# Moving and spreading the placing of a score table, with two score buffers, in a one-core recommendation kernel

## The reference, cut to what matters

```python
ub = jnp.concatenate([table_i1[rec_his[:, :, 0]], table_i2[rec_his[:, :, 1]], table_i3[rec_his[:, :, 2]]], axis=2)
mask = rec_his[:, :, 0] == 0
q = jnp.broadcast_to(item_emb[:, None, :], ub.shape)
att_in = jnp.concatenate([q, ub, q - ub, q * ub], axis=-1)
score = ((att_in @ w_att1.T + b_att1) @ w_att2.T + b_att2)[..., 0]
score = jnp.where(mask, 0.0, score)
browse = jnp.einsum('bl,ble->be', score, ub)
feat = jnp.concatenate([item_emb, browse, user_emb], axis=-1)
x = _dice(feat @ w1.T + b1, a1, g1, be1)      # _dice: mean and variance over the batch
x = _dice(x @ w2.T + b2, a2, g2, be2)
return jax.nn.sigmoid(x @ w3.T + b3)[:, 0]
```

## Time and profile before

| | us |
|---|---|
| three runs | 1587.96, 1591.98, 1605.28 |
| median | 1591.98 |
| the profiled execution, own time | 1586.62 |
| its span | 1584.8 |
| mean granted TensorE clock | 0.921 |
| DVE busy | 1438.4 (91%) |
| PE busy | 1328.5 (84%) |
| POOL busy | 1131.4 (71%) |
| ACT busy | 717.1 (45%) |

### The profile page before, as it was taken

One profiled execution on the slowest core, in us unless ns is written; L12 is line 12 of the kernel. 1 busy time (PEld: TensorE's weight loads), 2 busy tenths in 40 slices (PEclk: granted clock), 3 DMA queues, 4 the chain that ended last, 5 costly groups with the idle time before them and its releaser, 6 DMA issues.

```text
span 1584.8 us, 67332 instructions
## 1 busy us (share of the span) xinstructions
PE 1328.5 (84%) x26911; PEld 1224.4 (77%) x26911; DVE 1438.4 (91%) x1453; ACT 717.1 (45%) x1633; POOL 1131.4 (71%) x1669
## 2 busy tenths in 40 slices
PE   5687989889797988979788797888989798887965
PEld 4576878778796887869788797888879797787861
DVE  7799999999999898999989899898999999899955
ACT  5353544536354453525435353453535355352217
POOL 3588788787878787776766768587787878677830
PEclk8799999999899998999999899999999899898966
DMA  2778676675857686584676758567686856668730
GB/s 30 146 109 159 104 146 124 130 149 111 168 100 151 108 137 134 111 167 95 138 111 128 147 111 154 92 141 131 111 167 112 151 107 144 118 115 157 117 70 0
DMA packets 510281, 194.21 MB, mean 123 GB/s; under 512 B 484005, under 2 KB 491797, under 8 KB 510045
## 3 DMA queue, kind: packets, MB, share of 16 engines
q1 hardware_dynamic: 492454, 162.61, 57.2%
q10 hardware_dynamic: 15448, 26.51, 6.5%
q0 software_dynamic: 2144, 1.36, 0.8%
HBM read 8.45 MB, written 1.44 MB: 6 GB/s over the span
## 4 chain that ended last, share of the span: by engine, by line
POOL 58%; issue 24%; DVE 6%; PE 5%; DMA 2%; POOLq 2%; SPq 2%; ACT 1%; DVEq 0%; ACTq 0%
POOL score L431 16%; POOL score L436 13%; POOL score_r L440 10%; POOL parts L441 6%; POOL parts L444 6%; POOL parts L437 3%; POOL item_rows L409 2%; DMA hiT<-onehot_hi 2%; POOL user_rows L417 2%; PE sel L532 1%; DVE score_j L999 1%; DVE onehot_hi L967 1%; DVE scaled_lo L1011 1%; PE wsum_ps L549 1%; PE misc L637 1%
## 5 line engine op out<-in xcount | busy, mean ns | idle before, releaser
L532 PE MATMUL sel<-scoretab,hiT 128*128 128x75 bf16 x12288 | 560.3, 206 | 142.8 <-DMA hiT<-onehot_hi 116.8
L532 PEld LDWEIGHTS sel<-scoretab,hiT 128*128 128x128 bf16 x12288 | 521.3, 103 | 204.1 <-issue 147.2
L549 PE MATMUL wsum_ps<-scaled_lo,onehot_hi 100*128 100x75 bf16 x12288 | 554.3, 204 | 73.8 <-DVE scaled_lo L1011 73.7
L549 PEld LDWEIGHTS wsum_ps<-scaled_lo,onehot_hi 100*128 100x128 bf16 x12288 | 509.4, 102 | 89.9 <-DVE scaled_lo L1011 83.8
L1011 DVE TENSOR_TENSOR scaled_lo<-onehot_lo,parts 100x3744 bf16<-100x3744 bf16 x256 | 539.4, 2107 | 24.0 <-POOL parts L444 20.0
L754 ACT ACTIVATE wsum_ring<-wsum_ps 128x300 f32<-128x300 f32 x512 | 215.5, 421 | 674.7 <-PE wsum_ps L549 668.1
L431 POOL TENSOR_TENSOR score<-score_j 100x16 f32<-100x16 f32 x256 | 310.4, 1213 | 293.4 <-DVE score_j L999 292.6
L999 DVE TENSOR_REDUCE score_j<-sel 100x24 f32<-100x600 f32 x512 | 395.8, 773 | 34.7 <-PE sel L532 34.0
L967 DVE TENSOR_TENSOR onehot_hi<-digits,iota_hi 100x1920 bf16<-100x1920 bf16 x256 | 297.5, 1162 | 45.9 <-PE wsum_ps L549 45.4
L761 ACT ACTIVATE scores_b<-acc 128x512 bf16<-128x512 f32 (+1 forms) x318 | 256.1, 805 | 44.9 <-PE acc L568 23.7
L436 POOL TENSOR_TENSOR score<-score,score_j 100x16 f32<-100x16 f32 x256 | 229.7, 897 | 22.0
(11 more groups left out here) (155 smaller groups left out, 663.5 us busy)
## 6 DMA issues: line engine op xcount, KB each, us to landing
scoretab<-scores_b SPq DMA_DIRECT2D x144, 187.5 KB
weightsum<-wsum_ring ACTq DMA_DIRECT2D x128, 125.0 KB
weightsum<-wsum_ring ACTq DMA_DIRECT2D x64, 150.0 KB
scoretab<-scores_b SPq DMA_DIRECT2D x96, 93.8 KB
raw<-in_r_rec_his_dram SPq DMA_DIRECT2D x32, 150.0 KB
hiT<-onehot_hi SPq DMA_TRANSPOSE x256, 4.5
x_rows<-x_tile SPq DMA_DIRECT2D x14, 100.0 KB
scores_b<-x_rows SPq DMA_DIRECT2D x1, 1400.0 KB
```

The costliest lines, as they stand in the source:

```text
L532: mm = pe.matmul(sel[:, 2 * (s % 2) + q, (c % 4) * W:(c % 4 + 1) * W] .rearrange("p (j v) -> p j v", j=NF), hiT[0:HJ, s // 2 % 4, g * POSP ...
L549: mm = pe.matmul(wsum_ps[:, s % 2, b * W:(b + 1) * W].rearrange("p (j v) -> p j v", j=NF), hi_columns(ring_slot(n), g), scaled_lo[:, n % 2 ...
```

## The change

- The chunks are all 16 users (`CHUNK = 16`, eight a tile), and `scoretab` holds four of them in turn (`HELD = 4`, 64 users in all, half of what it held). Chunks 0 and 1 of tile t+1 are placed in steps 14 and 15 of tile t, and chunks 2 to 7 in steps 0, 2, 4, 6, 8 and 10 of tile t+1, each behind that step's transpose. This is 24 DMAs a tile in place of 15, with the same bytes.
- `scores_b` has two buffers, for even and odd tiles. ACT's first copy waits only for the chunks of the tile before.
- Splitting stands in slots 2 to 10 (rounds 0 to 2) and 16 to 27 (rounds 3 to 6), and not in slots 11 to 15. The last piece is in slot 27, as it was.
- PE's program is written out for all 16 tiles; SP and ACT loop over pairs of tiles, since the buffer alternates. DVE and POOL keep their loops.
- DVE clears half as many bytes ahead of tile 0 and fills the constant rows by 12 copies of 16 users in place of 6 of 64. In the tail two scratch tiles lie elsewhere.

```diff
-        scoretab_flat = sb("scoretab", [128, 2 * NF * HALF * 3 * LO], BF16)
+        scoretab_flat = sb("scoretab", [128, HELD * NF * CHUNK * 3 * LO], BF16)
-        scores_flat = sb("scores_b", [HJ, TILE * 3 * LO], BF16)
+        scores_flat = sb("scores_b", [HJ, 2 * TILE * 3 * LO], BF16)
...
-        ROWS = (0, 16, 32, 64, 96, 128)
-        CHUNKS = len(ROWS) - 1
         for r, (l0, l1) in enumerate(ROUNDS):
             for piece in ("all", 1, 2):
-                split_at[7 + len(split_at)] = (r, piece)
+                split_at[len(split_at) + (2 if r < 3 else 7)] = (r, piece)
...
-            def place_scores(t, c):
-                await_ge(split_copied, SPLIT_DONE * (t + 1))
-                b0, b1 = ROWS[c], ROWS[c + 1]
-                if isinstance(t, int) and t == 0:
-                    sp.wait_ge(scoretab_zero, b0 // HALF + 1)
+            def place_scores(t, c, odd):
+                g = CHUNKS * t + c
+                if c == 0:
+                    await_ge(split_copied, SPLIT_DONE * (t + 1))
+                if isinstance(g, int) and g < HELD:
+                    sp.wait_ge(scoretab_zero, c // 2 + 1)
                 else:
-                    await_ge(sel_full, SLOTS * t - (SLOTS - b1 // 4))
+                    await_ge(sel_full, (CHUNK // 4) * (g - HELD + 1))
...
-                    if n == 14 and not last:
-                        place_scores(t + 1, 0)
+                    if n >= 14 and not last:
+                        place_scores(t + 1, n - 14, 1 - odd)
                     if n + AHEAD < STEPS:
                         turn_hi(t, n + AHEAD)
                     elif not last:
                         turn_hi(t + 1, n + AHEAD - STEPS)
-                    if n < 2:
-                        place_scores(t, 3 + n)
+                    if n % 2 == 0 and n // 2 + 2 < CHUNKS:
+                        place_scores(t, n // 2 + 2, odd)
...
-            for c in range(3):
-                place_scores(0, c)
+            for c in range(2):
+                place_scores(0, c, 0)
...
-                if 4 * s in ROWS:
-                    pe.wait_ge(scoretab_in[ROWS.index(4 * s)], (t + 1) * (NF * 16))
+                chunk = 4 * s // CHUNK
+                if 4 * s % CHUNK == 0:
+                    pe.wait_ge(scoretab_in[chunk % HELD], (t * (CHUNKS // HELD) + (chunk // HELD + 1)) * (NF * 16))
...
-            with pe.Fori(0, (TILES - 2) // RUN) as run:
-                for i in range(RUN):
-                    for s in range(SLOTS):
-                        slot(run * RUN + (i + 1), s)
+            for t in range(TILES):
+                for s in range(SLOTS):
+                    slot(t, s, t % 2, last=t == TILES - 1)
...
-                        for c in range(CHUNKS):
-                            act.wait_ge(scoretab_in[c], (t + 1) * (NF * 16))
+                        for q in range(HELD):
+                            act.wait_ge(scoretab_in[q], t * ((CHUNKS // HELD) * (NF * 16)))
...
-            for hb in range(2):
-                dve.memset(scoretab_flat[:, hb * W * 3 * HALF:(hb + 1) * W * 3 * HALF].bitcast(F32), 0.0
-                           ).then_inc(scoretab_clear, 1)
+            half = (HELD // 2) * NF * CHUNK * 3 * LO
+            for h in range(2):
+                dve.memset(scoretab_flat[:, h * half:(h + 1) * half].bitcast(F32), 0.0).then_inc(scoretab_clear, 1)
```

More of the change, by code:

```diff
@@ L42, in build @@
     RING = 6
+    CHUNK = 16
+    CHUNKS = TILE // CHUNK
+    HELD = 4
     MH = H1 // 2
@@ L181, in build @@
         scoretab_clear = sem("scoretab_clear")
-        scoretab_in = [sem(f"scoretab_in{c}") for c in range(5)]
+        scoretab_in = [sem(f"scoretab_in{q}") for q in range(HELD)]
         weightsum_in = sem("weightsum_in")
@@ L372, in _ @@
                 turn_hi(0, n)
-            for c in range(3):
-                place_scores(0, c)
[L375 to L378, removed]
+            for c in range(2):
+                place_scores(0, c, 0)
+            tile(0, 0)
+            with sp.Fori(0, TILES // 2 - 1) as pair:
+                for odd in (1, 0):
+                    tile(pair * 2 + (2 - odd), odd)
+            tile(TILES - 1, 1, last=True)
             sp.wait_ge(head_copied, 8)
@@ L553, in add_scores, with split_piece @@
                 mm.then_inc(wsum_full, 1)
-            def split_piece(r, piece, copied, first=False):
+            def split_piece(r, piece, copied, odd, first=False):
                 o = split_bank(first, r)
@@ L654, in task, with slot @@
                     mm.then_inc(task_full, 1)
-            def slot(t, s, last=False):
+            def slot(t, s, odd, last=False):
                 read_scores(t, s)
@@ L693, in _ @@
                         pe.wait_ge(const_ready, 2)
-                    split_piece(r, stage if stage else "all", NR * (stage - 1) + r + 1 if stage else 0, first=True)
+                    split_piece(r, stage if stage else "all", NR * (stage - 1) + r + 1 if stage else 0, 0, first=True)
             pe.wait_ge(split_copied, 3 * NR)
-            for s in range(SLOTS):
-                slot(0, s)
-            with pe.Fori(0, (TILES - 2) // RUN) as run:
-                for i in range(RUN):
-                    for s in range(SLOTS):
-                        slot(run * RUN + (i + 1), s)
-            for s in range(SLOTS):
-                slot(TILES - 1, s, last=True)
+            for t in range(TILES):
+                for s in range(SLOTS):
+                    slot(t, s, t % 2, last=t == TILES - 1)
             for s in range(SLOTS - LAG, SLOTS):
@@ L909, in _ @@
                 for r in range(NR):
-                    split_copy(r, stage, NR * stage + r + 1, first=True)
+                    split_copy(r, stage, NR * stage + r + 1, 0, first=True)
             for s in range(SLOTS):
-                slot(0, s)
-            with act.Fori(1, TILES - 1) as t:
-                for s in range(SLOTS):
-                    slot(t, s)
+                slot(0, s, 0)
+            with act.Fori(0, TILES // 2 - 1) as pair:
+                for odd in (1, 0):
+                    for s in range(SLOTS):
+                        slot(pair * 2 + (2 - odd), s, odd)
             for s in range(SLOTS):
-                slot(TILES - 1, s, last=True)
+                slot(TILES - 1, s, 1, last=True)
             for s in range(SLOTS - LAG, SLOTS):
```

55 lines of the change are left out of this document (27 added, 28 removed).

## The result

The changed kernel takes 1529.46 us in the median of four runs (1527.79 to 1530.35), against 1593.57 for the kernel before in the same comparison. The ratio is 0.9587, with a 95% interval of 0.9532 to 0.9642. It is faster by 4.1%, and its runs lie within 3 us where those of before spread over 17. The profiled executions stand at 1586.62 and 1529.61, with spans of 1584.8 and 1527.6.

The account below looks back on a forecast made before the run. DVE's work was taken as the floor, its idle time caused by PE in most tiles, then POOL. 35 + 2 + 0 + 4 = 41 us off 1586.6 gave 1545.6, plus 2.7 for a 1548 median; range 1524 to 1584.

Parts of the forecast that it names:

- Tiles 1 to 14: DVE's idle time in these tiles falls from 5.93 to 3.4 us a tile, so 35 us go.
- Late transposes, then the low clock: Steps 3 and 4: PE waits 4.58 us, then works partly at 1.2 GHz; total transpose wait falls from 116.8 to some 60.
- The landing time: Transposes issued in steps 1 and 2: long landings of 9.7 us become common ones; the longest falls below 8.
- The load in slots 9 to 15: Lookup, finishing and splitting together make PE late, 0.76 us in step 6 of tile 9; either alone costs nothing.
- The cover of a transpose: Issued two steps, some 10.5 us, before its reader; a chunk's delay up to 2 us is free, 4 us makes PE late.
- POOL: Gathers in steps 1 to 3 are the limit behind PE; DVE's wait for POOL goes up from 20.0 to 30 or so.
- rival 3: Steps 3 to 8: POOL's wait replaces PE's, only tile 15 and the start are won: 1580; chance 0.12.
- Rival 1: PE and POOL both get out of the way, POOL's 2.2 us fall to about 1: about 1527; chance 0.15.
- The rule on coalescing: Nine more copies a tile: by this rule 16-user chunks move less well than 32-user ones and the DMA share rises.
- rival 2: Steps 4 to 10: 24 copies make transposes late all through the tile, PE late by 0.3 us: say 1580; chance 0.15.
- Ahead of tile 0: Less clearing and filling brings the first pick forward by 4 us, bounds 1 and 6, limited by ACT's last split copy.
- The step from own time to median: Profiled execution lies below the timed runs; half that distance, 2.7 us, was added to 1545.6 to give a median.

Follow-up runs that it names:

- run 2: Changed kernel plus six unread 187.5 KB copies to DRAM in steps 0 and 1 of every tile, its new splitting kept: 1569.34 us, ratio 0.9828.
- run 3: Changed kernel plus six unread 187.5 KB copies in steps 0 and 1, and splitting put back into slots 7 to 27: 1587.36 us, ratio 0.9971.
- run 6: Changed kernel plus three unread 187.5 KB copies to DRAM in step 0 alone of every tile: 1560.34 us, ratio 0.9834.
- Run 1: Changed kernel with splitting put back into slots 7 to 27, the spread placing and two score buffers kept: 1531.38 us, ratio 0.9609.
- run 10: Changed kernel with POOL's gathers moved to steps 5 to 7, 12 and 13, and splitting back in slots 7 to 27: 1519.45 us, ratio 0.9543.
- run 7: Changed kernel with 32-user chunks, two held, placed in steps 14, 0, 5 and 9, same bytes and splitting: 1575.61 us, ratio 0.9876.

## Why the prediction was right, and where it was not

The time lies in the range, with the forecast (1548) 19 us too high: the gain of 41 us was 57. By its steps:

*Tiles 1 to 14: 35 us taken, 48.5 measured.* This is the mis-sized term. I left 3.4 us of idle a tile and 2.74 stayed, which is 9 us. The other 4 are DVE's own time, taken as unchanged at 86.6 a tile: it fell from 1213.05 to 1209.21. Why it did is not shown. What I had left standing beside POOL's waits was PE's part at slot 16 (0.3 to 1.3 us in tiles 12 and 9). It was a remainder of the late start, not of the layer and the piece in that slot, and in tile 9 it went with the late start: step 8 is 5.30 us with the same work in it.

*Late transposes, then the low clock.* The late transposes are confirmed. The wait for them fell to 42.3, below the 60 forecast, and the clock is 1.00 in steps 2 to 8 of tile 9. The burst brings the late transposes and the low clock back together (runs 2, 3 and 6), so the clock's own share is not shown. The landing time was the wrong sign to read. The trace has landings for 128 of the 256 transposes, and the 9.7 us of the earlier trace rows is one transpose at 1504.44 in the last tile, behind the 1400 KB load, which I had not looked at. It has nothing to do with the burst, and in the changed kernel it is 10.2, not below 8. The transpose of the earlier trace rows has no recorded landing; PE begins its read 9.7 us after the issue began (890.55 to 900.27), by chance the same figure. For those issued in step 1 of tiles 1 to 14 the mean landing went from 5.9 to 4.2 us.

*The load in slots 9 to 15.* The step "both together cost 0.76 in step 6" took two readings for two causes of the same weight. Run 1 shows that they are not: some 2 us for the pause once the placing is spread, and nearly all else for the placing with its second buffer (the start gives 4). The comparison of tile 9's step 6 with tile 15's mixed the load with the lead that PE entered it with. Tile 12 could have told this from the trace of before: it had finishing and splitting in step 6 too, and only 0.8 us of waits for PE in the whole tile. The rule from runs 1, 3 and 10 is that PE is short of time in those slots, and that its lead pays for it if it is there.

*The cover of a transpose.* I gave 2 us of delay for free, and room for a chunk in steps 4 to 10. For 16 users that was right: steps 9 to 11 are no longer than 5.3 us. For 32 it is right in step 5 and wrong in step 9 (run 7).

*POOL.* The forecast of its wait, up from 20.0 to 30 or so, came out at 34.3, and rival 3's mechanism is there as a part: 14 us came up as PE's waits fell from 79.4 to 17.8. Rival 1 named nearly the right time for a wrong reason, since POOL's waits did not shrink. The times of rivals 2 and 3 lack the 2.7 us from own time to median that the forecast and rival 1 have (rival 3 would be 1583 and not 1580); nothing hangs on it.

*The rule on coalescing.* The Trainium skill, page "DMA: Bandwidth & Descriptors", section "Rules for kernel authors", says to coalesce many small transfers, and gives 64 KB as the size under which one pays mostly overhead. Both sizes here lie above that (93.8 and 187.5 KB), so the figure does not choose between them. In run 7 the version with larger copies is 46 us slower, though it places them in other steps too. They share SP's queue with transposes that PE waits for, and what counts here is what one of them puts in front of the next transpose.

*Ahead of tile 0: 4 taken, 4.3 measured*, with the bound at ACT's last split copy right. *Tile 15: 2 taken, 3.3 measured. Tile 0: 0 taken, 1.1 won. The step from own time to median: 2.7 added, none there.* The spread of the runs is gone too, with the stalls.

## What to carry to other kernels

When a latency-bound transfer and bulk copies share a DMA queue, cut the bulk and issue each piece right behind the urgent transfer, all through the period; check every piece against the other traffic of its step. Before moving a transfer later, look at who waits for its buffer to come free. An engine that is late in a crowded stretch may have lost its lead earlier: compare the same stretch in a tile that entered it in time before blaming the load. When the outer limit is gone, look at once for the one behind it: moving POOL's gathers brought nothing before this change and 16 us after it.

## What the runs showed that I had not expected

- Three extra copies in one step cost 31 us and six in two steps 40; halving a burst keeps most of its price.
- Taking 30 us out of PE's wait for transposes (116.8 to 87.0) brought nothing, since the same edit made PE wait 30.2 us for ACT, which waited for the one score buffer.
- Runs spread over 17 us before and over 3 after: the tiles of the changed kernel are nearly all 89.0 us long, where they were 89.8 to 95.0.
